# Building the adjacency blocks of a graph layer with three destination nodes to a PSUM column, read back as bytes

## The reference

```python
def _gcn_conv(x, W, row, col, n_nodes):
    xl = x @ W.T
    deg = jax.ops.segment_sum(ones, col, num_segments=n_nodes)
    dis = jnp.where(deg > 0, deg ** (-0.5), 0.0)
    norm = dis[row] * dis[col]
    msg = xl[row] * norm[:, None]
    return jax.ops.segment_sum(msg, col, num_segments=n_nodes)
...
row = jnp.concatenate([es[0], loops])          # every node is its own neighbour too
col = jnp.concatenate([es[1], loops])
h = relu(batchnorm(_gcn_conv(layernorm(x), W1, row, col)))
x = x + relu(batchnorm(_gcn_conv(h, W2, row, col)) + layernorm(x))
x = x + ffn(layernorm(x))                      # 8 experts, the likeliest one per row
```

## Time and profile before

| | |
|---|---|
| time, median of 3 runs | 1975.37 us (1975.32 to 1977.41) |
| profiled execution, first to last instruction (span) | 1689.5 us |
| the median less this span: what lies around the program's instructions | 285.9 us |
| preparation, until PE's dense matmuls begin | 0 to 141.6 us |
| first convolution's neighbour sums, with the building of all blocks | 141.6 to about 610 us |
| linear layers and batch norm | about 610 to 780 us |
| second convolution's neighbour sums | about 780 to 1200 us |
| the rest (feed-forward layer) | about 1200 to 1689.5 us |

### The profile page before, as it was taken

How to read it: one execution, slowest core, us unless ns; L and a number is a source line. 1 busy time by engine, 2 the same in 40 slices (tenths; PEclk the granted TensorE clock), 3 DMA queues, 4 the chain that set the end, 5 groups by cost and what they waited for, 6 DMA issues and landing times. The chain is left out here.

```text
span 1689.5 us, 32733 instructions
## 1 busy us (share of the span) xinstructions
PE 1476.3 (87%) x10003; PEld 1029.7 (61%) x10004; DVE 1092.0 (65%) x3900; ACT 851.9 (50%) x1611; POOL 1036.4 (61%) x1139
## 2 busy tenths in 40 slices
PE   0137999999999989798999999999779999949998
PEld 0114666666666669796665555556565666627776
DVE  6578888888888747683233343443386778767775
ACT  0555555555555535574234432222288787725665
POOL 5745677777777710244777777777222566636776
PEclk9999999999999999899999999999899999959999
DMA  7727666666666610046988999998489343489992
GB/s 242 205 96 262 200 202 206 208 204 207 204 205 211 208 55 0 23 163 232 322 287 297 323 316 325 325 325 286 125 278 355 147 172 134 181 223 270 260 282 75
DMA packets 219570, 364.80 MB, mean 216 GB/s; under 512 B 31416, under 2 KB 146551, under 8 KB 219174
## 3 DMA queue, kind: packets, MB, share of 16 engines
q1 hardware_dynamic: 158202, 217.62, 39.1%
q0 software_dynamic: 46816, 131.61, 24.7%
q10 hardware_dynamic: 14412, 13.86, 3.2%
HBM read 240.34 MB, written 130.12 MB: 219 GB/s over the span
## 5 line engine op out<-in xcount | busy, mean ns | idle before, releaser
L1181 POOL DMA_INDIRECT grows<-table_dram,gsrc x680 | 657.3, 967 | 247.2 <-issue 214.3
L1113 PE MATMUL ps<-table,adj 128*128 128x512 f16 x2842 | 705.1, 380 | 4.2 <-PEq L1330 4.2
L1113 PEld LDWEIGHTS ps<-table,adj 128*128 128x128 f16 x2842 | 389.4, 142 | 166.0 <-issue 8.1
L857 ACT ACTIVATE adj<-ps 128x490 f16<-128x490 f32 (+1 forms) x390 | 223.9, 574 | 178.7 <-PE ps L842 174.6
L829 DVE TENSOR_SCALAR oh_k<-iota_k,keyrem 128x246 f16<-128x246 f16 x780 | 238.5, 310 | 0.0
L828 DVE TENSOR_SCALAR oh_r<-iota_r,keyrem 128x128 f16<-128x128 f16 x780 | 213.7, 275 | 4.0 <-ACT keyrem L352 3.7
L1062 PE MATMUL ps<-grows,oh_g 128*128 128x512 f16 x680 | 167.8, 381 | 16.5 <-DMA grows<-table_dram,gsrc 16.4
L842 PE MATMUL ps<-oh_k,oh_r 128*128 128x245 f16 x780 | 148.5, 273 | 17.4 <-DVE oh_k L829 13.7
L2399 PE MATMUL ps<-wd,h_hi 128*128 x896 | 152.7, 276 | 9.0 <-DVE h_lo L2446 9.0
L842 PEld LDWEIGHTS ps<-oh_k,oh_r 128*128 128x128 f16 x780 | 75.5, 98 | 94.8 <-DVE oh_k L829 20.0
L934 DVE SCALAR_TENSOR_TENSOR tmp_d<-ps,disP,tmp_d 128x256 f32<-128x256 f32 x30 | 14.5, 484 | 182.5 <-ACT tmp_d L1140 182.5
(11 more groups left out here) (379 smaller groups left out, 2710.7 us busy)
## 6 DMA issues: line engine op xcount, KB each, us to landing
kept<-sorted_h SPq DMA_DIRECT2D x224, 128.0 KB, 5.8
adj_dram<-adj SPq DMA_DIRECT2D x60, 367.5 KB
adj<-adj_dram SPq DMA_DIRECT2D x56, 367.5 KB, 7.3
cv_raw<-fwd SPq DMA_DIRECT2D x64, 256.0 KB, 5.7
adj_dram<-adj SPq DMA_DIRECT2D x30, 477.8 KB
adj<-adj_dram SPq DMA_DIRECT2D x28, 477.8 KB, 5.5
table_dram<-table SPq DMA_DIRECT2D x13, 896.0 KB, 4.1
grows<-table_dram,gsrc POOLq DMA_INDIRECT x680, 3.5
```

What stands on the lines that cost most here:

```text
L857: act.activation(m.adj[:, q % 3, d0:d0 + wide, :].rearrange("r d c -> r (d c)"), m.ps[:, n % 3, 0:wide * NT], ACT.Copy).then_inc(a.s_adj, 1)
L1113: last = pe.matmul(acc, adj[:, :, c], table[:, c, :], start=c == 0, stop=c == NT - 1)
L1181: pool.indirect_dma_start(m.grows[:, n % GR, j, :], None, m.table_dram, bass.IndirectOffsetOnAxis(ap=m.gsrc[:, g, part * BT + j:part * BT ...
```

## The change

Edges carry weights, so that one column of the product counts for three destination nodes at once. The place of a destination in its group of 15 nodes (now three windows of 5, ROLES = 3) is split into a column of three (place // 3) and a digit (0, 1, 2). The entry of `oh_k` is 2^-8, 1 or 2^8 by the digit (is_equal, then times the weight), and partition 127, which no edge uses any more, adds 2^15 to every column. The sum's mantissa then holds the three counts in three separate bytes, and ACT reads the float32 bank as bytes (stride 4 along the source blocks) and writes the same float16 counts to `adj` as before.

- A window now touches 2 or 3 columns of three: 98, 147 or 98 keys of the group's 245 (`SPAN`). The second and the third window share 49 keys with the one ahead of them, so their product is split in two matmuls, one that adds to what is there and one that begins new columns.
- A block is 26 windows in 9 groups (8 of three windows, one of two) in place of 13 groups; a step builds 10 groups in place of 14, at c = 0, 4, ... 36; the rings are 4 groups of one-hots in place of 6 (three windows each).
- `prepare` gets a third plane of `keyrem` (the weights) and nine DVE instructions that work out column, digit, validity and weight; ACT turns chunk and low byte to float32 apart (`chunkf`, `lowf`); POOL sets up a small table; DVE fills the constant partitions of the one-hot buffers at the start. Five groups (75 destinations) are made before the last `count`, four behind the table.

```diff
+PACK = 3
+BASEONE, SHIFT = float(1 << 15), 8
+ROLES = 3
+SPAN = ((0, 2 * NT), (NT, 4 * NT), (3 * NT, 5 * NT))
+NWIN = -(-P // WIN)
+GPB = -(-NWIN // ROLES)
+SPOTS = (0, 1, 3, 4, 6, 7, 9, 10, 12, 13)
+AHEAD = len(SPOTS)
-GPB = WB // 2
-OHR = 6
+OHR = 4
-AHEAD = 14
...
+        dve.memset(m.agg.oh_r[96:P, :, :, :], 1.0)
+        dve.memset(m.agg.oh_k[96:P, :, :, NT:], BASEONE)
+        dve.memset(m.agg.oh_k[96:P, :, 0, 0:NT], BASEONE)
+        link(dve.memset(m.agg.oh_k[96:P, :, 1:, 0:NT], 0.0))
...
+        for h in range(2):
+            for b in range(ROLES):
+                pool.memset(full[:, :, b, h], 1.0 + WIN * ((b + h * WJ) % ROLES)).then_inc(s_group, 1)
+            pool.memset(in_group[:, WJ - 1:WJ, h], 1.0 + WIN * ((WJ - 1 + h * WJ) % ROLES)).then_inc(s_group, 1)
+        pool.iota(odd[:, :], [[0, 1]], base=0, channel_multiplier=1).then_inc(s_group, 1)
         pool.wait_ge(s_rows, 16)
...
         dve.wait_ge(s_edges, 16 * WJ)
-        link(dve.tensor_tensor(keyw[:, :, :], halves_of(edges[:, :, :])[:, :, :, 1], w5[:, :].unsqueeze(2).to_broadcast([WP, WJ, P]), ALU.subtract))
-        dve.scalar_tensor_tensor(keyw[:, :, :], keyw[:, :, :], float(NT), bytes_of(edges[:, :, :])[:, :, :, 1], ALU.mult, ALU.add).then_inc(s_keyw, 1)
-        dve.wait_ge(s_keys, NB)
-        for n in range(BEFORE // 2):
+        dve.wait_ge(s_group, 9)
+        link(dve.tensor_scalar(odd[:, :], odd[:, :], 1, None, ALU.bitwise_and))
+        link(dve.tensor_copy(oddf[:, :], odd[:, :]))
+        link(dve.tensor_scalar(w5[:, :], w5[:, :], oddf[:, 0:1], None, ALU.add))
+        dve.tensor_tensor(keyw[:, :, :], halves_of(edges[:, :, :])[:, :, :, 1], w5[:, :].unsqueeze(2).to_broadcast([WP, WJ, P]), ALU.subtract).then_inc(s_keyw, 1)
+        dve.wait_ge(s_keys, 2)
...
+        dve.wait_ge(s_keys, 4)
...
+        dve.wait_ge(s_keys, 2 * PACK)
+        for n in range(FIRST):
             one_hots(dve, m, n)
         count(len(EARLY) + 1)
...
 def one_hots(dve, m, n):
...
-    for i in range(2):
...
-        dve.tensor_scalar(a.oh_r[:, n % OHR, i, :], m.iota_r[:, :], m.keyrem[:, 1, j, w:w + 1], None, ALU.is_equal)
-        last = dve.tensor_scalar(a.oh_k[:, n % OHR, i, :], m.iota_k[:, :], m.keyrem[:, 0, j, w:w + 1], None, ALU.is_equal)
+    for i in windows_of(g):
...
+        dve.tensor_scalar(a.oh_r[some, n % OHR, i % ROLES, :], m.iota_r[some, :], m.keyrem[some, 1, j, w:w + 1], None, ALU.is_equal)
+        last = dve.tensor_scalar(a.oh_k[some, n % OHR, i % ROLES, 0:c1 - c0], m.iota_k[some, c0:c1], m.keyrem[some, 0, j, w:w + 1],
+                                 m.keyrem[some, 2, j, w:w + 1], ALU.is_equal, ALU.mult)
...
 def build_group(pe, m, n):
...
+    for i in windows_of(g):
+        rows, keys, (c0, c1) = a.oh_r[:, n % OHR, i % ROLES, :], a.oh_k[:, n % OHR, i % ROLES, :], span(i)
+        if made > c0:
+            pe.matmul(bank[:, c0:made], rows, keys[:, 0:made - c0], start=False, stop=True)
+        last = pe.matmul(bank[:, made:c1], rows, keys[:, made - c0:c1 - c0], start=True, stop=i == windows_of(g)[-1])
+        made = c1
...
 def keep_built(act, m, n):
...
+    counts = m.ps[:, n % 3, 0:KEYS].bitcast(U8).rearrange("r (g c k) -> r g k c", c=NT, k=4)
...
+    last = act.activation(to(0, whole, PACK), counts[:, 0:whole, 0:PACK, :], ACT.Copy)
...
-                if c % 3 == 0 and c // 3 < len(groups):
-                    build_group(pe, m, groups[c // 3])
+                if c % 4 == 0 and c // 4 < len(groups):
+                    build_group(pe, m, groups[c // 4])
```

More of the change, by code:

```diff
@@ L126, in small @@
             return take(name, [P, *shape], dt)
-        m.keyrem = small("keyrem", [2, WJ, WP], F32)
+        m.keyrem = small("keyrem", [3, WJ, WP], F32)
+        m.tile_tab = m.at("tile_tab", take.next, [P, 2, 64], I32)
         m.gsrc = small("gsrc", [NG, TPG], I32)
@@ L270, in prepare @@
     assert take.next <= m.r3 + 37632 + GR * BT * 4 * C
+    take = Place(m, m.r1 + 31232)
+    slot_c, slot_s, chunk_t = (take(n, [P, WJ, WP], F16) for n in ("slot_c", "slot_s", "chunk_t"))
+    third, digit, valid = (take(n, [P, WJ, WP], F16) for n in ("third", "digit", "valid"))
+    rounded, bits = take("rounded", [P, WJ, WP], F32), take("bits", [P, WJ, WP], F32)
+    in_group, odd, oddf = take("in_group", [P, WJ, 2], F16), take("odd", [WP, 1], I32), take("oddf", [WP, 1], F32)
+    assert take.next <= m.r2
     take = Place(m, m.work)
@@ L663, in window, with at_spot @@
     half, j = divmod(w, WJ)
-    return half, j, min(WIN, HALF - WIN * j)
+    return half, j, min(WIN, P - WIN * w)
+def at_spot(groups, g):
+    return [groups[SPOTS.index(g)]] if g in SPOTS and SPOTS.index(g) < len(groups) else []
 def aggregate_tensors(m):
@@ L672, in aggregate_tensors @@
     x_at = take.next
-    a.oh_r, a.oh_k = take("oh_r", [P, OHR, 2, P], F16), take("oh_k", [P, OHR, 2, KEYS + 1], F16)
-    take = Place(m, x_at)
+    a.oh_r, a.oh_k = take("oh_r", [P, OHR, ROLES, P], F16), take("oh_k", [P, OHR, ROLES, 3 * NT], F16)
+    take = Place(m, m.r5 + PARTR * 2048)
     a.idl = take("x_idl", [P, P], F16)
@@ L816, in convert, with windows_of, span @@
     return load, store, high, low, first
+def windows_of(g):
+    return range(ROLES * g, min(ROLES * (g + 1), NWIN))
+def span(w):
+    c0, c1 = SPAN[w % ROLES]
+    last = WIN * (w % ROLES) + window(w)[2] - 1
+    return c0, min(c1, (last // PACK + 1) * NT)
 def one_hots(dve, m, n):
@@ L838, in build_group @@
         pe.wait_ge(a.s_adj, n - 2)
-    at = 0
-    for i in range(2):
-        keys = window(2 * g + i)[2] * NT
-        last = pe.matmul(m.ps[:, n % 3, at:at + keys], a.oh_r[:, n % OHR, i, :], a.oh_k[:, n % OHR, i, 0:keys],
-                         start=True, stop=True)
-        at += keys
+    bank, made = m.ps[:, n % 3, :], 0
+    for i in windows_of(g):
[4 more added lines that the diff above has]
+        made = c1
     last.then_inc(a.s_build, 1)
@@ L947, in v_main @@
             groups = groups_of(k - 1) if not second else ()
-            for g in range(AHEAD):
-                if g < len(groups):
-                    one_hots(dve, m, groups[g])
-                    loops_after(dve, m, groups[g])
-                if not second and k == LASTLOOP and g == AHEAD - 1:
+            for g in range(STEPS):
+                for n in at_spot(groups, g):
+                    one_hots(dve, m, n)
+                    loops_after(dve, m, n)
+                if not second and k == LASTLOOP and g == STEPS - 1:
                     for piece in (2, 3):
@@ L1159, in a_main @@
                         a_gather_lo(act, q)
[L1160 to L1161 removed]
+                for n in at_spot(groups, g):
+                    keep_built(act, m, n)
                 if g == 4 and 0 <= k - 2 < nd:
```

91 lines of the change are left out of this document (54 added, 37 removed).

## The result

The changed kernel takes 1996.07 us (median of 4, 1990.57 to 2005.39), and the kernel before, beside it, 1975.34. The ratio is 1.0102, with a 95 % interval of 1.0069 to 1.0135: slower by 1 %, where 1967 us was forecast and the range ended at 1974.

The account below looks back on a forecast made before the run. PE bounds the kernel by only about 6.8 us, then POOL. First gather 142.4 + 450.2 + 1.5 wait puts the last dense block at 601.1 instead of 609.6; 1689.5 - 8.5 + 285.9 gives 1967 us, range 1960 to 1974.

Parts of the forecast that it names:

- the sum's frame: Whole program: profiled span 1689.5 us less 8.5, plus 285.9 us taken to lie around the span and stay.
- POOL becomes the bound: First convolution: POOL's gathers need 450.2 us, so some 26 us of PE's saving become waits for gathers; chance 0.72.
- PE's work: First convolution: 261 groups of five matmuls at 0.164 us replace 377 pairs (81.1 us), 38.3 us less.
- rival 1: Building matmuls: narrow ones go at the early rate, 0.29 us a group, PE stays the bound; 1973 us, chance 0.07.
- rival 2: Building matmuls: weight load not hidden, each of five pays it in full; 0.49 us a group, 2025 us, chance 0.04.
- rival 3: ACT's copies: reading bytes from PSUM is slow, decisive from 2.3 ns an element; near 2200 us, chance 0.05.
- DVE's part of the forecast: Preparation, DVE between the edges and the last count: 3.4 us longer.
- (a): Preparation: DVE fills 3300 columns per partition of constants before the edges arrive; taken as 1.0 us.
- (b): Preparation: POOL's eight small fills and an iota stand ahead of the `edges` gathers; 0.6 us.
- the digits: Preparation: DVE's nine instructions over 780 elements, taken as 7.2 us (bounds 4.2 and 9.1).
- rival 4: Preparation grows by more than 11.8 us, DVE's long operations holding up POOL's gathers; 1975 to 1980 us, chance 0.06.
- I cost this at nothing, since PE will have 26 us to spare: First convolution: one-hots only 4 groups ahead of PE, DVE's identity pieces waiting for a copy three groups back; 0 us.

Follow-up runs that it names:

- prompt signals: In both kernels POOL issued all `near` gathers ahead of the `edges` gathers; ratio 1.0143 for the changed kernel, 1.0069 for the kernel before.
- The later turn: Gathered block's turn moved from c = 20 to c = 32, with ACT's copy, first convolution: changed kernel 1996.84 us (0.996), kernel before 1994.11 us (0.9944).
- that of the second: Second profile of the kernel before, run again unchanged: span 2000.9 us; measured time 2004.02 us, ratio to itself 1.0003.

## Why the prediction was wrong

- **The step that failed** is the sum's frame: "with the 285.9 us around it (the median of the runs less the span, taken to stay)". They lie inside the program, as pauses in the three stages with gathers; 1.8 us lie around it. The number alone should have stopped the argument. The Trainium skill, "Runtime: NRT & Kernel Launch", section "The ~15µs preamble/postamble breakdown", gives about 6.2 us by which a profile's total exceeds the reported time; here the span lies 1.8 us below the time, so size and sign differ, but neither figure is near 286. All that followed took the schedule of an execution without pauses for that of the timed ones.
- **"POOL becomes the bound", with some 26 us of PE's saving lost to waits for gathers**: not so. No wait of PE is put down to the landing of a gather. POOL waits for PE (25 times, 139.6 us), PE for ACT's copies, and ACT for PE's late signals. In these executions the gain does not stop at 8.5 us: with half of the building matmuls gone the kernel before gained 37 (32 by the medians). Whether POOL would be the bound in an execution without pauses, no run shows.
- **PE's work** was sized right: 0.17 us a group for 0.164, so 377 x 0.215 - 261 x 0.17 = 36.7 us for the 38.3 forecast (PE's busy time in the stage falls by 24 to 27). The 81 ns of the Trainium skill, "TensorE: Matmul & The Clock Gate", section "Back-to-back issue gap", for a matmul of 128 columns (five of them 0.405 us) were rightly passed over: 0.034 each in the row at 412.98, for 49 and 98 columns. Rivals 1, 2 and 3 fell: 0.29 a group, an unhidden weight load, and 2.3 ns an element for the copy were all not seen (0.17, and 0.788/735 = 1.1 ns).
- **The preparation**: DVE's part of the forecast, 3.4 us, is 3.04 with prompt signals. (a) and (b) cost nothing, since POOL's `edges` gathers start at 80.95 us against 81.81; the digits are 6.1 us for 7.2. As the kernel stands the last count comes 9 to 10.5 us later than before and PE 10 to 12. This is rival 4 by its place (it asked for more than 11.8 us), but not by its mechanism ("DVE's long operations holding up POOL's gathers"): POOL's gathers hold up PE's signals, and the third plane and the digits put two more of these on the path.
- **"I cost this at nothing, since PE will have 26 us to spare"** was the other wrong step: round trips through ACT are most of what PE stands for in the stage (105 of 154 us by name in the result's profile). The account by the profiles: 10 to 12 us more in the preparation; in the stage PE is busy for 24 to 27 us less and idle for 23 to 41 more, with 36 to 49 more at the turn of the gathered block, 13 to 17 more at the turn of the dense block and 31 to 35 less at the building groups. That is 6 to 30 us in all; by the medians it is 20.7 and 23.6. The later turn gives the changed kernel 18 us more than the kernel before, which is most of it.

What stays open: why the change moves PE's stop from the building groups to the turn. It was argued that four dense matmuls to a group let PE run on to c = 20 before it needs a late copy; but with groups at every third place the stops went to the building groups and the other turn and grew, and that order, with no group behind c = 27, is not the one of before either. And no run shows why the first profiled execution had no pauses, with the same gathers, nor what in POOL's issuing delays PE's signals. Nor is it shown that recording has no part in it: for DVE's 390 signals that a group's one-hots are made the trace of the first profile holds 390 update records, that of the second 265.

## What to carry to other kernels

Before a sum is made, the profile's span and the time must agree; where they do not, the profile is of another schedule than the one that is timed, and only prices of single operations may be taken from it. Where one engine's signals are late while another issues gathers, count the round trips between engines rather than busy time, and give each the longest distance to its use that the order allows: moving one turn by twelve matmuls was worth 29 us here, about as much as the change takes off PE. A handoff that was added to a chain beside a run of gathers cost 6 to 7.5 us by lateness here, beside 3 us by its own length.

## What the runs showed of the hardware

- PE's signals were up to 13 us late while POOL issued indirect gathers back to back, and came within 0.1 us when no gather was in flight; at the two places shown ACT's own signals were not late. Gathers alone do not do it: in the first profile none of ACT's waits in the stage is `remote`.
- The Trainium skill, "DMA: Bandwidth & Descriptors", section "Anatomy of one DMA — SWDGE (gpsimd) path", puts a semaphore update at about 100 ns; it speaks of a DMA's own, and the waits of 8 to 9 us above are of another order.
- DVE too was held up without waiting for anything: its 49 small `bn_aggr` instructions, one behind the other, had 16 pauses of 0.2 to 1.9 us between 47 and 68 us; POOL's run of `near` gathers ended at 62.2 us, some 5 us before the last of them. A longer run (the `near` gathers all first) went with 31 pauses and moved the next counts from 73 to 90 us. In the first profile the 49 instructions have no pause, beside the same gathers. DVE's waits in the result's profile, 40 to 80 us, and the instructions in the first:

```profile
DVE ln_mv L555 <- issue: 17.6, 16, 1.9
```

```profile
45.94 3.33 DVE L528 BATCH_NORM_AGGREGATE ln_mv<-ln_st 128x2 f32<-128x6 f32 x49
```

- PE's granted clock is 1.00 through the stage of the first profile and 0.88 to 0.89 in the timed ones: the stops cost a second time, as 509 us of busy time for the work of 468.
